# One fused attention and gated-MLP kernel: the first attention's product with v, from 64 calls over 32 partitions to 32 calls over 128, with v copied across partitions

## What is computed

```python
# first block (16 heads of 16 features, no mask)
xn = rms_norm(x, g_norm) * (1.0 + scale) + shift          # scale, shift: one per sequence
q, k, v = heads_of(xn @ W_qkv)
q, k = rms_norm(q, g_q), rms_norm(k, g_k)
attn = softmax(einsum('bhqd,bhkd->bhqk', q, k) * d ** (-0.5))
o = einsum('bhqk,bhkd->bhqd', attn, v)                     # "a" attention
y = o + o @ W_out
# second block
attn2 = causal_attention(rmsnorm(y, ln1_w), Wq, Wk, Wv, Wo)  # "b" attention
mod = 0.1 * tanh(attn2 @ A)
h = rmsnorm(y, ln2_w)
gate = silu(h @ W_in.T + mod * (h @ A) @ B)
out = x + y + (gate * (h @ W_up.T)) @ W_down.T
```

## Time and profile before

| | |
|---|---|
| median of 3 runs | 677.26 us (672.82, 677.26, 684.4) |
| the profiled execution, its own time | 674.3 us |
| span of that execution in the trace | 672.5 us |
| mean granted TensorE clock, as a share of full speed | 0.954 |
| PE busy with matmuls | 599.9 us, 89% |
| PE busy with weight loads | 553.0 us, 82% |
| DVE busy | 461.7 us, 69% |
| ACT busy | 368.7 us, 55% |
| POOL busy | 218.4 us, 32% |

### The profile page before, as it was taken

How to read it: one execution, slowest core, us unless ns; L and a number is a source line. 1 busy time by engine, 2 the same in 40 slices (tenths; PEclk the granted TensorE clock), 3 DMA queues, 4 the chain that set the end, 5 groups by cost and what they waited for, 6 DMA issues and landing times.

```text
span 672.5 us, 22378 instructions
## 1 busy us (share of the span) xinstructions
PE 599.9 (89%) x9056; PEld 553.0 (82%) x9056; DVE 461.7 (69%) x1074; ACT 368.7 (55%) x770; POOL 218.4 (32%) x196
## 2 busy tenths in 40 slices
PE   2345569999999999999999999999999999997987
PEld 2334459998998989998999899998998899996887
DVE  3465867778686777777786867686777778684532
ACT  2354537565565748374656657483747466562412
POOL 0121132515143433425151524334251506141213
PEclk9755979999999999999999999999999999998989
DMA  5142010111101010111011010101111110101000
GB/s 155 48 153 68 21 40 2 35 32 34 34 18 50 12 55 9 27 34 32 33 33 33 18 49 14 53 9 27 35 31 32 34 32 19 34 15 35 8 26 17
DMA packets 40151, 24.32 MB, mean 36 GB/s; under 512 B 24016, under 2 KB 38992, under 8 KB 40064
## 3 DMA queue, kind: packets, MB, share of 16 engines
q1 hardware_dynamic: 40064, 23.02, 12.4%
HBM read 14.61 MB, written 4.19 MB: 28 GB/s over the span
## 4 chain that ended last, share of the span: by engine, by line
PE 66%; SPq 14%; DVE 7%; ACT 4%; DMA 4%; issue 3%; POOL 1%; POOLq 0%; ACTq 0%; DVEq 0%
SPq L338 14%; PE gate_bank L387 11%; PE up_bank L387 9%; PE b_banks L387 7%; PE down_bank L581 7%; PE a_banks L379 7%; PE x_bank L379 5%; PE b_banks L379 4%; PE a_banks L472 4%; PE b_banks L399 2%; DMA vj<-vs 2%; PE gate_bank L567 2%; PE b_banks L534 2%; PE a_banks L399 2%; PE x_bank L490 1%
## 5 line engine op out<-in xcount | busy, mean ns | idle before, releaser
L979 POOL TENSOR_TENSOR qk<-qk,rx 128x512 f32<-128x512 f32 x32 | 34.3, 1092 | 229.4 <-DVE rx L783 229.4
L991 POOL TENSOR_TENSOR gl<-gu,gh 128x512 fp32r<-128x512 f32 x64 | 81.6, 1285 | 70.5 <-ACT gh L735 70.5
L387 PE MATMUL up_bank<-uh,wup_hi 128*128 128x256 f32 x256 | 78.7, 307 | 0.7 <-DVE gu L885 0.7
L387 PE MATMUL gate_bank<-uh,win_hi 128*128 128x256 f32 x256 | 75.0, 293 | 0.3
L387 PE MATMUL up_bank<-ul,wup_hi 128*128 128x256 f32 x256 | 72.9, 285 | 0.0
L387 PE MATMUL up_bank<-uh,wup_lo 128*128 128x256 f32 x256 | 72.7, 284 | 0.0
L581 PE MATMUL down_bank<-wdn_hi,gh 128*128 128x256 f32 x256 | 71.9, 281 | 0.7 <-POOL gl L991 0.7
L581 PE MATMUL down_bank<-wdn_hi,gl 128*128 128x256 f32 x256 | 72.1, 282 | 0.0
L581 PE MATMUL down_bank<-wdn_lo,gh 128*128 128x256 f32 x256 | 72.0, 281 | 0.0
L387 PE MATMUL gate_bank<-ul,win_hi 128*128 128x256 f32 x256 | 71.7, 280 | 0.0
L387 PE MATMUL gate_bank<-uh,win_lo 128*128 128x256 f32 x256 | 71.6, 280 | 0.0
(11 more groups left out here) (153 smaller groups left out, 1811.7 us busy)
## 6 DMA issues: line engine op xcount, KB each, us to landing
xa<-in_x SPq DMA_DIRECT2D x16, 256.0 KB, 2.8
xres<-in_x SPq DMA_DIRECT2D x16, 256.0 KB, 2.9
vj<-vs SPq DMA_DIRECT2D x256, 16.0 KB, 1.8
out<-outb SPq DMA_DIRECT2D x16, 256.0 KB, 3.2
stage<-in_w_inT SPq DMA_DIRECT2D x2, 512.0 KB, 4.0
stage<-in_w_upT SPq DMA_DIRECT2D x2, 512.0 KB, 3.7
stage<-in_w_downT SPq DMA_DIRECT2D x2, 512.0 KB, 4.0
stage<-in_w_qkv SPq DMA_DIRECT2D x2, 384.0 KB, 3.7
```

Of the source, the lines that this page charges most:

```text
L387: mm = pe.matmul(dst, w[a][:, k, c0:c0 + P], mov[b][:, k, :], start=(first and k == 0 and j == 0), stop=(last and k == KT - 1 and j == 2), ...
L979: pool.tensor_tensor(heads_of, heads_of, rx[:, 32 * t:32 * t + 32].unsqueeze(2).to_broadcast([P, 2 * H, HD]), ALU.mult).then_inc(done[name ...
L991: pool.tensor_tensor(gl[:, c % 2], gu[:, c % 2], gh[:, c % 2].bitcast(F32), ALU.subtract).then_inc(f_lo, 1)
```

## The change

The first attention gets the layout of the second. `a_scores` now places heads as `b_scores` did (one function `scores`, the place functions are gone). v gets a buffer `vd` of 128 partitions x [tile, sequence, 64 features, 4 heads of a group], zeroed once by POOL. `a_v_out` becomes two steps: `a_v_out0` on ACT copies for sequences 0 and 1, `a_v_out1` on DVE for 2 and 3, in eight copies each; a copy takes 32 partitions of `x_bank` to another 32 partitions of `vd`, 128 elements on each. The 64 columns of a call hold the 16 features of one head in each strip, with zeros where a strip belongs to another head, so that the product comes out complete and in place; `omask`, `o1`, `o_odd` and `o_even` are gone, and `o_hi` and `o_lo` read PSUM directly. To get that order of features, the hi and lo splits of W_qkv at the start write permuted columns (three pieces where there was one). `cT` and `mblk` now share memory with other buffers. `ORDER` is written anew: 116 steps, its start at another step. `WEIGHTS_AT`, which says where the loads and splits of later weights stand in the first periods, is written anew too.

```diff
-    ("x_load", 2), ("m_mul", -1), ("a_pv0", 0), ("m_turn", -1), ("x_scale", 1), ("a_pv1", 0), ("m_out", -1),
...
+    ("m_turn", -1), ("x_scale", 1), ("a_pv", 0), ("m_out", -1), ("x_shift", 1), ("f_gate0", -1), ("o_hi", 0),
...
+        vd = sb("vd", [P, TB, 4, 4 * HD, 4])
...
+                st = st.rearrange("p (s h u d) -> p s h u d", s=3, h=4, d=HD)
+                return [(st[:, i], *(w[:, k, i * D:(i + 1) * D].rearrange(order, u=4, d=HD) for w in wqkv), 1.0)
+                        for i, order in enumerate(2 * ["p (u h d) -> p h u d"] + ["p (u d h) -> p h u d"])]
...
+        def v_strip(b, u):
+
+            j = (u + b) % 4
+            cols = slice(4 * HD * u, 4 * HD * u + 4 * HD)
+            return (vd[32 * j:32 * j + 32, :, b, HD * u:HD * u + HD].rearrange("p t d h -> p t (d h)"),
+                    by_tile(Xb)[32 * b:32 * b + 32, :, cols])
...
-            def a_place(t, m, b, g):
-                c = t * 256 + m * P
-                return Ab[32 * b:32 * b + 32, g, c:c + P]
...
+                                j = (2 * m + g + b) % 4
+                                c = (b // 2) * 256 + t * P
+                                mm = pe.matmul(banks[32 * j:32 * j + 32, b % 2, c:c + P], stat(t, m)[rows, 32 * b:32 * b + 32],
...
-                elif name in ("a_pv0", "a_pv1"):
...
-                                    mm = pe.matmul(Ab[32 * r:32 * r + 32, b // 2, c:c + 64], vs1[rows, t, hd:hd + 32],
-                                                   pTa[rows, t, hz:hz + 2, :].rearrange("p h s -> p (h s)"),
-                                                   start=True, stop=True, skip_group_check=True)
+                elif name == "a_pv":
...
                     for t in range(TB):
+                        for b in range(4):
+                            for h in range(4):
+                                rows = slice(64 * (h % 2), 64 * (h % 2) + 64)
+                                c = t * P + b * S
+                                hz = 4 * (2 * (b % 2) + b // 2) + h
+                                mm = pe.matmul(Ab[rows, h // 2, c:c + S], vd[:, t, b, :, h], pTa[:, t, hz, :],
+                                               start=True, stop=True, skip_group_check=True)
...
-                    act.activation(vs1[:, :, :].rearrange("p t d -> p (t d)"), Xb[:, :], ACT.Copy).then_inc(done[name], 1)
+                    for b in range(2):
+                        for u in range(4):
+                            to, of = v_strip(b, u)
+                            ins = act.activation(to, of, ACT.Copy)
+                    ins.then_inc(done[name], 1)
...
-                    act.activation(by_token(oh), by_seq_first(o1), ACT.Copy).then_inc(done[name], 1)
+                    act.activation(oh[:, :, :], Ab[:, :, 0:BLOCK], ACT.Copy).then_inc(done[name], 1)
...
+                elif name == "a_v_out1":
...
+                    for b in range(2, 4):
+                        for u in range(4):
+                            to, of = v_strip(b, u)
+                            ins = dve.tensor_copy(to, of)
+                    ins.then_inc(done[name], 1)
...
-                    dve.tensor_tensor(by_token(ol), by_seq_first(o1), by_token(oh).bitcast(F32),
+                    dve.tensor_tensor(ol[:, :, :], Ab[:, :, 0:BLOCK], oh[:, :, :].bitcast(F32),
...
+            pool.memset(vd[:, :, :, :, :], 0.0).then_inc(vd_zeroed, 1)
```

More of the change, by code:

```diff
@@ L35 @@
 ORDER = [
-    ("x_load", 2), ("m_mul", -1), ("a_pv0", 0), ("m_turn", -1), ("x_scale", 1), ("a_pv1", 0), ("m_out", -1),
-    ("x_shift", 1), ("f_gate0", -1), ("o_odd", 0), ("o_even", 0), ("x_hi", 1), ("f_down3", -2), ("x_lo", 1),
-    ("o_hi", 0), ("f_tanh0", -1), ("o_lo", 0), ("f_half0", -1), ("r_mm", 0), ("f_mul0", -1), ("f_out", -2),
-    ("a_qk0", 1), ("r_square", 0), ("r_load", 0), ("f_store", -2), ("a_qk1", 1), ("r_rms", 0), ("x_square", 2),
[14 rows of a table removed]
[10 rows of a table added]
+    ("m_turn", -1), ("x_scale", 1), ("a_pv", 0), ("m_out", -1), ("x_shift", 1), ("f_gate0", -1), ("o_hi", 0),
+    ("o_lo", 0), ("f_out", -2), ("r_mm", 0), ("f_tanh0", -1), ("r_load", 0), ("x_hi", 1), ("f_store", -2),
[6 rows of a table added]
 ]
@@ L62 @@
 SHIFT = dict(ORDER)
[L63 to L64 removed]
+X_BANK_READERS = {"x_turn": ["x_scale"], "a_v": ["a_v_out0", "a_v_out1"], "r_turn": ["r_lo"],
+                  "b_v0": ["b_v_out0"], "b_v1": ["b_v_out1"]}
+X_BANK_ORDER = [name for name, _ in ORDER if name in X_BANK_READERS]
 PIECES = [("qkv0", 768), ("qkv1", 768), ("w_out", 512), ("q2", 512), ("k2", 512), ("a2", 32),
@@ L160, in bass_adaln_attention_ffn @@
         Db = ctx.enter_context(nc.psum_tensor("down_bank", [P, 512], F32))
-        done = {name: sem(name) for name, _ in ORDER if name[:2] != "f_" and name[2:] not in ("load", "move")}
+        done = {name: sem(name) for name, _ in ORDER if name[:2] != "f_" and name[2:] != "load" and name != "b_move"}
         f_up, f_gate, f_tanh, f_half, f_mul, f_hi, f_lo, f_down, f_out = (
@@ L206, in wait_x_bank @@
                 if not isinstance(n, int) or 0 <= m < NB:
-                    wait(pe, done[X_BANK_READER[before]], m)
+                    for reader in X_BANK_READERS[before]:
+                        wait(pe, done[reader], m)
                     return
@@ L390, in feature_major, with scores @@
                 return mm
-            def scores(place, stat, mov, start):
+            def scores(banks, stat, mov, start):
                 for t in range(TB):
@@ L427, in do @@
                     wait(pe, done["x_lo"], n)
-                    wait(pe, done["o_odd"], n - 1)
-                    wait(pe, done["o_even"], n - 1)
+                    wait(pe, done["o_hi"], n - 1)
+                    wait(pe, done["o_lo"], n - 1)
                     if isinstance(n, int) and n == 0:
@@ L668, in do @@
                     act.activation(za[:, t], za[:, t], ACT.Exp).then_inc(done[name], 1)
-                elif name == "o_odd":
-                    wait(act, done["a_pv1"], n)
-                    wait(act, done["o_lo"], n - 1)
-                    act.activation(o1[:, :, :], outputs_of(Ab, 1), ACT.Copy, scale=omask[:, 1:2]).then_inc(done[name], 1)
                 elif name == "o_hi":
-                    wait(act, done["o_even"], n)
+                    wait(act, done["a_pv"], n)
                     wait(act, done["r_mm"], n - 1)
-                    act.activation(by_token(oh), by_seq_first(o1), ACT.Copy).then_inc(done[name], 1)
+                    act.activation(oh[:, :, :], Ab[:, :, 0:BLOCK], ACT.Copy).then_inc(done[name], 1)
                 elif name == "r_square":
@@ L803, in softmax @@
                     wait(dve, done[f"{x}_weigh{t}"], n)
-                    wait(dve, done["a_pv1" if x == "a" else "b_pv"], n - 1)
+                    wait(dve, done[f"{x}_pv"], n - 1)
                     dve.transpose(pT[:, t].rearrange("p h s -> p (h s)"),
@@ L955, in _ @@
             dve.wait_ge(v2_loaded, 64)
-            for n_own, mask in ((2, omask), (4, kmask)):
-                own = heads[:, :].rearrange("p (a h) -> p h a", h=n_own)
-                ins = dve.tensor_reduce(mask[:, :], own, AX_X, ALU.add)
-            ins.then_inc(prep, 1)
+            dve.tensor_reduce(kmask[:, :], heads[:, :].rearrange("p (a h) -> p h a", h=4), AX_X, ALU.add).then_inc(prep, 1)
             run(dve, do, weights)
```

92 lines of the change are left out of this document (35 added, 57 removed), and 30 rows, old and new, of the table ORDER.

## The result

| | before | after |
|---|---|---|
| median | 675.26 us (672.82 to 684.4, 4 runs) | **716.35 us** (714.68 to 717.11, 4 runs) |
| ratio | | 1.062 (95%: 1.057 to 1.067) |
| span of the profiled execution | 672.5 us | 715.3 us |
| granted clock | 0.954 | 0.950 |

The change makes the kernel 6.2% slower, 41 us. The forecast was 670 us, with 653 to 686 as the range: wrong in size and in sign.

A forecast was written before the change was run, and what follows sets the result against it. PE's own work was taken to bound the steady period. Periods -5.3 us (0.24 - 0.2 - 0.42, some 14 times), slips +2.8, end -3, start -1: -6.5 from 674.3 to 667.8, as a median 670 us; range 653 to 686.

The forecast's parts named there:

- PE, the product: a_pv on PE: 64 wide calls take 1.8 us where two steps took 1.56, +0.24 us a block (-0.25 to +1.06).
- A: Rival on the product: a call's cost doesn't depend on its columns; product 0.78 us, median 654 us; chance 0.13.
- C: Rival on the product: wide tiles don't overlap load and stream; product 2.62 us, median 683 us; chance 0.12.
- B: Rival: DVE ends last between b_scores and product through copies and m_mul; +17 to +28 us, median 685 to 695; chance 0.13.
- both stretches: DVE against PE from b_scores to the product: 9.2 us against 9.2, then 7.1 against 7.3; 0.2 us to spare.
- slips: Allowance for DVE's tight path: 0.2 us a period, +2.8 us over 14 periods.
- POOL's `f_lo2`: Behind ACT's copies and f_hi2: f_lo2 comes about when PE gets to f_down2; 1.5 late if copies take 3.2 us.
- The DMA race: b_move's DMAs against b_pv: with b_scores in the stretch, PE's wait goes, -0.42 us a period.
- -3 at the end: Last blocks: b_pv's longest waits for vj shrink with 1.5 us more PE work between, 3 us less.
- D: Rival: nothing is gained from the DMA race, the queue slowed by something moving with it; +6 us, 676; chance 0.12.
- `r_mm`'s wait for `ol`: PE order: o_hi and o_lo alone, about 1.4 us, fit under f_gate0, so the wait goes, -0.2 us a period.
- Start: First blocks and weights: -1.45 us without o_odd and o_even, about 0.5 added by split pieces; -1 us, give or take 4.

The follow-up runs named there:

- run 5: The changed kernel with the product's 64 weight columns 8 bytes apart in vd, each copy of v made two of half the size: 694.74 us.
- run 1: The changed kernel with the product's 64 weight columns side by side in vd instead of 16 bytes apart: 685.41 us, 1.016 of before.
- run 2: The changed kernel with each 64-column call of the product cut into two 32-column calls, columns still 16 bytes apart: 686.83 us.
- run 3: The changed kernel with columns side by side and two 32-column calls for each 64-column call of the product: 677.3 us.
- run 6: The changed kernel, columns still 16 bytes apart, with m_mul put back behind the flips and m_turn behind a_pv: 714.19 us.
- run 7: The changed kernel with columns side by side, 32-column calls, m_mul back behind the flips and m_turn behind a_pv: 666.78 us, 0.985 of before.
- run 8: As run 7, with only one in eight copies of v on ACT and on DVE, so output is not the reference's: 659.88 us.
- run 9: The kernel before with only ORDER changed: b_v1 ahead of b_scores, b_v_out1 and b_move right behind f_tanh2: 662.27 us, 0.980 of before.
- run 4: The kernel before with its product's 32 stationary columns taken 16 bytes apart, output not the reference's: 676.1 us, beside 674.83 of before.
- run 10: The kernel before with m_mul moved ahead of a_flip1 and a_flip0: 696.67 us.

## Why the prediction was wrong

**PE, the product: wrong, and this is the step that failed.** On record: "I take 1.8 us", between 1.31 and 2.62, so +0.24 us a block. Measured: 4.03, +2.47 a block, 39.5 us over 16 blocks. The step halved the 105 ns of the 128-column load and had both halves load at once; it took the load to go with the number of columns alone. All three rows it stood on had weights whose columns lie side by side, and the change's own line, `vd[:, t, b, :, h]`, has them 16 bytes apart. The upper bound came from those rows as well, so the range couldn't hold the answer. What the runs put in its place is in the table. "In its strip" is the product's time, times the strips, divided by its instructions, and so has the end of the step in it; "start to start" is the median distance between two instructions of one strip, which has not:

| columns | apart | strips at once | in its strip | start to start | product |
|---|---|---|---|---|---|
| 64 | 16 bytes | 2 | 126 ns | 120 ns | 4.03 us (after) |
| 64 | 8 bytes | 2 | 66 ns | 60 ns | 2.11 us (run 5) |
| 64 | side by side | 2 | 64 ns | 58 ns | 2.06 us (run 1) |
| 32 | 16 bytes | 4 | 67 ns | 60 ns | 2.15 us (run 2) |
| 32 | side by side | 4 | 40 ns | 33 ns | 1.29 us (run 3) |

Even side by side it is 2.06, not 1.8: an instruction has a little more than half of the wide one's time, 64 against 52.5 ns. That alone would have been 4 us; the stride was 31. That the two halves work at once was right: run 1 has 32 ns for an instruction, less than the 52.5 ns that half of the wide row would take alone. They do so in after too: its weight loads start 34 and 86 ns apart by turns, and each record lasts 216, so it is the load that is slower and not the halves that take turns.

The Trainium skill ("TensorE: Matmul & The Clock Gate", LDWEIGHTS) has the load take the number of columns divided by 1.2 in ns; an estimate by it is 53.3 ns for 64. The rows differ: 58 ns from start to start side by side, and 120 ns at 16 bytes for the same number, so the measurement decides, and the rule holds at most for weights without such a stride.

**The rivals on the product.** A (0.78 us) is refuted: an instruction's time goes with its columns, their spacing and its strips, from 10.1 ns to 63 ns each. C (2.62 us, 681) had the right direction and was too small; at side by side the truth lies between C and my value.

**DVE: late, by what B named.** On record: both stretches "just fit, with 0.2 us to spare", with 0.2 us allowed for slips, and B deciding from 0.2 us a copy. The timeline of DVE in after, with POOL's and SP's:

```profile
360.24 0.69 DVE L775 TENSOR_REDUCE mxb<-b_banks 128x16 f32<-128x512 f32 x1 [0.96 <-PE b_banks L397]
...
365.46 2.42 DVE L830 COPY vd<-x_bank 32x128 f32<-32x128 f32 x8
...
370.46 0.68 DVE L775 TENSOR_REDUCE mxa<-a_banks 128x16 f32<-128x512 f32 x1
...
374.82 0.43 DVE L856 SCALAR_TENSOR_TENSOR m<-th,vs 128x32 f32<-128x32 f32 x1
375.28 0.96 DVE L859 CAST mt<-m 128x32 fp32r<-128x32 f32 x1
...
376.47 1.30 DVE L789 STREAM_TRANSPOSE pTa<-za 128x512 f32<-128x512 f32 x2
```

```profile
374.15 2.06 POOL L976 TENSOR_TENSOR za<-za,ria 128x512 f32<-128x512 f32 x2 [0.80 <-DVE ria L785]
```

```profile
359.23 11.06 SPq L334 DMA_DIRECT2D vj<-vs  x16
```

The first stretch, 360.24 to 370.46, is 10.2 us where 9.2 was reckoned; the copies have 0.8 of the 1.0 over, 0.30 us each and not 0.2. The second, 370.46 to 377.77, is 7.3 where 7.1 was reckoned, with `m_mul` at 1.65 and not 1.2. Together 1.2 over, 0.2 of it covered, and the product waits 0.73. So B's mechanism is real, at less than its price (11 us over the kernel, it had 17 to 28). Putting `m_mul` and `m_turn` back removes the product's wait with all the copies in place (runs 6 and 7). Whether fewer or cheaper copies alone would have done it, with `m_mul` where the change has it, wasn't run; run 8 shows only that they still cost 0.3 us a period behind run 7.

**POOL's `f_lo2`: under-priced.** I had it come "about when PE gets to `f_down2`", at no cost. It comes 0.36 us late in each period, and run 8 ties most of that to the copies: with one in eight, 3 waits are left of 14.

**The DMA race: right.** The issues start at 359.23 and end at 370.29, the last lands 1.8 us later, at about 372.1, and `b_pv` starts at 373.44: won by 1.3 us. Forecast were -0.42 us a period and -3 at the end; run 9 alone has -0.5 in each of the first 14 periods and -4.7 in the last one and behind it, some of that from the clock. In after the end shows nothing of the -3 (27.3 us behind the last `b_pv` where it was 27.1). D is refuted by both. Its price was also reckoned too low: without the -3 at the end it is 679, not 676.

**`r_mm`'s wait for `ol`: right for after,** where 14 of 15 waits are gone. But it doesn't hold by `f_gate0` alone, as reckoned: with `m_mul` and `m_turn` put back, 12 waits are there (run 7, 3.3 us beside the 1.6 at the start).

**Start: wrong in sign.** -1 us was taken, give or take 4, and it is +4. The copies stand in the chain of a lone block (8 x 0.27 on ACT, 8 x 0.30 on DVE), which the prediction had counted for DVE's steady state and not there. Run 8 gets 3.9 us back.

**The sum, remade** with the measured sizes, a period: product +2.47, `pTa` +0.73, `f_lo2` +0.36, `vj` -0.67, `ol` -0.2, together +2.69 against 2.57 measured, or 40.4 in 15 periods against 38.5; with +4.1 and +0.2 at the ends 44.7 against 42.8. (On record, 667.8 scaled to the median is 670.7 and not 670; it changes nothing.)

## What to carry to other kernels

Look at the layout of a matmul's stationary operand in memory, not only at its shape: when a row of the profile is to give the price of a load, it must have the same distance between columns as well as the same number of them. Where a kernel is bound by one engine, price a change by its dearest part alone and ask whether the part that pays (here a list with the DMAs earlier, 13 us) can be had without it. And fewer instructions are no gain where each holds a larger part of the array: 128 small loads in four strips took 1.29 us, 64 wide ones in two 2.06.

## What the runs showed of the hardware

- float32 weights 16 bytes apart load at about half speed: 120 ns against 58 from start to start in a strip, 4.03 us against 2.06 for the product (64 columns), and 60 ns against 33, 2.15 us against 1.29 (32 columns). 8 bytes apart, 60 ns and 2.11 us, they don't. Why the step lies there wasn't measured; distances of more than 16 bytes weren't tried.
- The same stride costs only 0.08 us a step in the product of before, 32x32 tiles with 64 streaming columns (run 4), though its load records grow from 107 ns to 143.
- Some small DVE instructions are held until POOL's running one ends. The cast of 32 columns takes 0.18 us in before and in runs 6 and 7, behind the flips, and 0.96 in after, ahead of them; there it starts at 375.28 and ends at 376.24, POOL's `za` at 376.21. DVE's `rsa` reduction (0.63 us at 373.99) isn't held by the same `za`. The tile's instruction in after (min/median/max), then in run 7:

```profile
L859 DVE CAST mt<-m x16: 182/964/966, 98.1 to 689.2; 128x32 fp32r<-128x32 f32 x16
```

```profile
L860 DVE CAST mt<-m x16: 181/182/182, 98.0 to 640.5; 128x32 fp32r<-128x32 f32 x16
```

  In run 10 it is the multiplication `m` that is held, 1.07 us where it takes 0.15 in run 7, to 0.05 us behind POOL's end. In before `m` was held too, 0.66 us from 350.53, beside this one on POOL:

```profile
349.84 1.29 POOL L991 TENSOR_TENSOR gl<-gu,gh 128x512 fp32r<-128x512 f32 x1
```

  So the 1.2 us that the prediction took for `m_mul` had half a us of this in it already. The hold agrees with the Trainium skill ("SBUF — State Buffer", SBUF: two separate sides), by which DVE and GpSimd share one pair of ports as an exclusive lock for a whole instruction, for a DVE instruction in a two-port mode or with two SBUF inputs. That it is this lock, and not another cause with the same timing, no run here isolates.
- The granted clock fell for some 3 us in each of six periods of run 6, which are about 1.3 us longer for it, in a kernel that keeps PE busy for 91% of the span, with no wait of PE over 0.3 us ahead of them; why there and not in run 7, where the 13 periods between the first and the last have 1.00, stays open. In before it fell three times behind the first period, at 607.9, 621.6 and 645.5, each time beside a wait of PE of 2.2 to 2.6 us, and not behind the waits of 0.5 to 1.1 us between. But run 9 has a wait of 2.6 us at its end too, ahead of 612.7, and no fall with it, so the wait alone doesn't decide it.
